# VectorE's second zero point of context rows ahead of the split of the maxima (iterations 9 to 15)

## What is computed

```python
x = x + attn(layernorm(x), Wq, Wk, Wv, Wo)       # 32 query heads, 8 key heads of 32, causal, softmax
x = x + fake_quant(layernorm(x)) @ fake_quant(ctx)  # ctx: 2 x 1024 x 1024
x = x + q8_8_linear(layernorm(x), weight, bias)

def fake_quant(x, scale, zp):
    q = clip(round(x / scale + zp), 0, 255)
    return (q - zp) * scale
```

## Time and profile before

| | us |
|---|---|
| median of 3 runs (480.33 to 484.75) | 481.57 |
| the profiled execution, its time | 483.82 |
| its span, first to last instruction | 481.9 |
| TensorE busy | 438.9 |
| VectorE busy | 379.4 |
| ScalarE busy | 299.4 |
| GpSimd busy | 288.4 |

### The profile page before, as it was taken

One profiled execution on the slowest core, in us unless ns is written; L12 is line 12 of the kernel. 1 busy time (PEld: TensorE's weight loads), 2 busy tenths in 40 slices (PEclk: granted clock), 3 DMA queues, 4 the chain that ended last, 5 costly groups with the idle time before them and its releaser, 6 DMA issues.

```text
span 481.9 us, 9721 instructions
## 1 busy us (share of the span) xinstructions
PE 438.9 (91%) x3730; PEld 241.3 (50%) x3730; DVE 379.4 (79%) x961; ACT 299.4 (62%) x302; POOL 288.4 (60%) x157
## 2 busy tenths in 40 slices
PE   0799997998899999999999999998998999899886
PEld 0676453545455555555554555445543444446442
DVE  5899862978888989888978888888287468799775
ACT  3775262223778777778777797779744312797632
POOL 5002662144899999999987877879730980707000
PEclk9999998999999999999999999999999999999999
DMA  8663486412231111110153213332177010000044
GB/s 332 215 220 110 147 277 199 174 45 79 78 123 32 47 47 55 57 50 31 47 176 111 81 37 107 111 110 94 40 275 264 30 38 29 1 1 2 2 177 177
DMA packets 21042, 50.93 MB, mean 106 GB/s; under 512 B 4736, under 2 KB 10112, under 8 KB 19712
## 3 DMA queue, kind: packets, MB, share of 16 engines
q1 hardware_dynamic: 19696, 41.79, 25.4%
q10 hardware_dynamic: 1296, 8.45, 5.0%
HBM read 40.67 MB, written 9.44 MB: 104 GB/s over the span
## 4 chain that ended last, share of the span: by engine, by line
PE 50%; DVE 21%; POOL 12%; ACT 7%; issue 5%; DMA 5%; SPq 0%; ACTq 0%; DVEq 0%; POOLq 0%
PE ps L1466 11%; PE ps L1372 8%; PE ps L1289 8%; PE ps L1617 5%; PE ps L1353 5%; PE ps L1334 4%; POOL more L1206 4%; DVE stat L769 3%; ACT s1reg L566 3%; POOL s1reg L1206 3%; POOL wkv L1206 2%; PE ps L1572 2%; PE ps L1355 2%; DVE qstack L957 2%; DVE ps L829 2%
## 5 line engine op out<-in xcount | busy, mean ns | idle before, releaser
L829 DVE CUSTOM_DVE_ANT_0 ps<-ps,causal 128x512 f32<-128x512 f32 (+3 forms) x256 | 120.4, 511 | 19.3 <-PE ps L1334 17.3
L566 ACT ACTIVATE s1reg<-ps 128x1280 f32<-128x1280 f32 x64 | 78.8, 1231 | 48.5 <-PE ps L1355 48.5
L1289 PE MATMUL ps<-xT,wqx 128*128 128x512 f16 x384 | 96.5, 384 | 0.0
L1466 PE MATMUL ps<-wo_reg,xT 128*128 128x512 f16 x384 | 93.0, 379 | 0.0
L1334 PE MATMUL ps<-kreg,qstack 96*128 96x512 f16 (+3 forms) x256 | 60.5, 301 | 10.0 <-DVE mt L829 6.7
L1353 PE MATMUL ps<-qstack,kreg 98*128 98x512 f16 (+3 forms) x256 | 57.2, 301 | 0.5 <-ACT s1reg L566 0.5
L1289 PEld LDWEIGHTS ps<-xT,wqx 128*128 128x128 f16 x384 | 37.2, 99 | 37.3 <-issue 2.2
L1466 PEld LDWEIGHTS ps<-wo_reg,xT 128*128 128x128 f16 x384 | 36.5, 97 | 36.6 <-issue 0.2
L1187 POOL TENSOR_TENSOR s1reg<-s1reg 128x512 f32<-128x512 f32 x11 | 16.0, 1451 | 63.0 <-DVE s1reg L818 62.9
L1206 POOL TENSOR_TENSOR s1reg<-s1reg 128x1280 f16<-128x1280 f32 x19 | 49.8, 2622 | 6.2 <-ACT s1reg L572 6.0
L1206 POOL TENSOR_TENSOR wkv<-s1reg,wkv 128x1280 f16<-128x1280 f32 x18 | 47.2, 2628 | 7.5 <-ACT wkv L572 7.5
(11 more groups left out here) (134 smaller groups left out, 929.1 us busy)
## 6 DMA issues: line engine op xcount, KB each, us to landing
s1reg<-in_weights ACTq DMA_DIRECT2D x8, 1024.0 KB, 5.1
s1reg<-in_ctx SPq DMA_DIRECT2D x16, 512.0 KB, 4.2
qstack<-rope_scratch SPq DMA_DIRECT2D x48, 128.0 KB, 2.6
rope_scratch<-s1reg SPq DMA_DIRECT2D x40, 128.0 KB, 2.2
qstack<-in_x SPq DMA_DIRECT2D x8, 512.0 KB, 5.4
s1reg<-in_x SPq DMA_DIRECT2D x16, 256.0 KB, 3.1
out<-s1reg SPq DMA_DIRECT2D x7, 512.0 KB, 2.7
s1reg<-in_L_ffn_weight SPq DMA_DIRECT2D x5, 512.0 KB, 6.0
```

The source lines that it names most:

```text
L566: nc.scalar.activation(ebuf[:, j % 2, :], st_ps[:, 0:SCORES], ACT.Exp, scale=EXP_SCALE, bias=P_LOG_SCALE).then_inc(e_done, 1)
L829: last = nc.vector.tensor_tensor_reduce(part, part, causal[:, T - w:T], 1.0, LOWEST, ALU.add, ALU.max, mt[:, G % 2, h, qt:qt + 1])
L1289: last = mm(out_ap, w(ws, k), xT[:, xs, KT * b + k, :], start=(k == 0 and n == 0), stop=(k == KT - 1 and n == 2))
L1466: last = mm(ps[:, bank, :], xT[:, os, KT * b + k, t], wo_sb[:, ws, 4 * h:4 * h + 4, k, :], start=(k == 0 and n == 0), stop=(k == KT - 1 an ...
```

## The change

In the loop of VectorE the zero point of the even tile, with its two waits, goes from behind maximum 6 to ahead of the split. No instruction is added or removed, and the other engines' instructions and waits are the same.

```diff
                 maxes(G, 3, 6)
-                if G < NG - 1:
-                    split_max(G + 1)
-                maxes(G, 6, 7)
                 if g >= 1:
                     dve.wait_ge(st_done, G * 4)
                     ctx(g * 2 - 2, 0)
-                maxes(G, 7, 11)
+                if G < NG - 1:
+                    split_max(G + 1)
+                maxes(G, 6, 11)
```

## The result

The changed kernel takes 480.41 us (median of 21 runs, 477.39 to 483.22), the kernel before 483.16 us (21 runs, 479.95 to 485.86). The ratio, which is worked out from the single runs and is not the quotient of the two medians, is 0.9948, with a 95% interval of 0.9926 to 0.9970: 2.5 us faster, between 1.4 and 3.6; the medians differ by 2.75. One run of the third, 521.49 us at a granted clock of 0.85 where all others had 0.99 to 1.00, is left out of its median and ratio.

The account below looks back on a forecast made before the run. VectorE's even zero point, waiting for GpSimd, was taken to hold up TensorE. 0.73 + 4 x 0.65 to 0.72 + 0 to 0.1 gave 3.3 to 3.7, taken as 3.4 us: 478.2 from 481.57; 8 in 10: 475.9 to 480.6.

Parts of the forecast that it names:

- What bounds the kernel: VectorE's even zero point waits for GpSimd's low half and holds the maxima TensorE needs; 15.04 us an iteration.
- V: Landmark of each iteration: the start of the denominators on TensorE; V to V was 15.04 us.
- The zero point takes 0.74 in its new place, the split costs nothing: VectorE, iterations 9 to 13: zero point starts before GpSimd, 0.74 us instead of 1.55; split 0.16 late, cost nothing.
- The slower rival: Zero point comes after GpSimd has started its low half; unit 10 1.38 us later, 6.9 us in all, 488.5; chance 0.04.
- The ring of 14.32 or 14.39 us: V, exponential 2, ScalarE's run, GpSimd's last low half, V again: limits each iteration's gain to 0.65 to 0.72 us.
- The full gain: Rival: V does not hang on the low halves, so TensorE's 5.0 us all arrive, 476.6 us; chance 0.14.
- The 0.07: Extra time of TensorE's denominators after a wait, 1.27 against 1.20 us, added to 14.32 to give 14.39.
- The odd zero point: VectorE's unmoved zero point: takes about 1.4 us instead of 0.74, priced at 0 to 0.1 us an iteration.
- the chain over L566, L572 and L1205: Sign in the profile after: the chain in 260 to 330 us runs over these lines in place of L957.
- V(9) to V(10), 0.73: First step: V(10) can't be before 261.57 because of GpSimd's last low half, so it gains 0.73 us, not 1.20.
- TensorE alone needs 14.09: TensorE's iteration without waiting for GpSimd: 15.04 less 0.95 us gained at unit 10.
- From the stage to the predicted time: Whole kernel: 3.4 us gained between V(9) and V(15), taken from the median of 481.57, gives 478.2 us.

Follow-up runs that it names:

- the third: The changed kernel measured a third time, with no further edit, beside the kernel before: 479.61 against 482.88 us, ratio 0.9922.
- the second profile of before: The kernel before measured against itself, nothing changed: 483.40 against 482.88 us, ratio 1.0016.
- the heads alone: Kernel before with ScalarE's high half of the head outputs moved behind exponential 3's high half from iteration 9 on: 483.66 against 481.97 us, ratio 1.0039.
- the two repeats: The changed kernel measured again twice, no further edit, against the kernel before: ratios 0.9963 and 0.9922.

## Where the prediction was right, and where it was not

*What bounds the kernel:* right. The zero point at its old place waited for the low half; shown by moving it behind the split (15.69 us from V to V), and by shortening the low half in place (14.40).

*The zero point takes 0.74 in its new place, the split costs nothing:* right, 0.75, and maximum 6 still waits 0.30 for TensorE. The slower rival's mechanism is real (2.62 us, 15.69), but its condition was not met: the zero point comes 0.56 us ahead of the low half (284.49 and 285.05).

*The ring of 14.32 or 14.39 us:* right, 14.40 measured in each of the iterations. The full gain did not come because of this ring: 0.38 us of TensorE's gain became a wait for GpSimd. The 0.07 between the two sums is no cost of a wait, though. It is the difference of the two landmarks named above:

```profile
277.27 0.39 PE L1372 MATMUL ps<-more,ones_h 128*32 128x512 f16 x1
```

Counted from this first matmul, exponential 2 (283.13) came 5.86 us after V(11) before the change too, and the 32 matmuls take 1.27 us with and without a wait ahead of them. So the ring is 5.86 + 5.56 + 2.62 + 0.35 = 14.39. The odd zero point's 1.48 (1.4 expected) and the chain over L566, L572 and L1205 are as written.

*V(9) to V(10), 0.73:* mis-sized, by what was taken as the step before. It was 15.46 in the profile of before, in which ScalarE's bytes waited for their transfer; the prediction kept the last low half where that wait had put it. The row of ScalarE's timeline of before, after which exponential 2 came 6.30 us after V(9) and not 5.86:

```profile
251.92 1.24 ACT L585 ACTIVATE wkv<-s1reg,qs 128x1024 uint8<-128x1024 f32 x1 [0.41 <-DMA s1reg<-in_ctx]
```

In the second profile of before there was no such wait, and the step took 15.04; with the heads alone the wait was 0.25 and the step 15.30. After the change it took 14.40, and 14.51 in its third run. The term is worth 0.5 to 1.1 us, depending on the execution, and the sum of the stage 3.2 to 3.7 us: 3.3 to 3.7 had been forecast.

*TensorE alone needs 14.09:* wrong by 0.14 (13.95). Up to unit 8 (10.69 us after V(11)) TensorE's iteration is the same before and after, so nothing came from exponential 0; all of it came at units 9 and 10. Maximum 8 started 0.42 us behind unit 8 (287.68 and 287.26) and not 0.53, and unit 10 followed unit 9 directly, 1.09 us earlier after V than before where 0.95 was worked out. This would have made the full gain larger; it didn't touch the forecast.

*From the stage to the predicted time:* this is the step that failed, in two terms. The first is the size: 3.4 us off a base of 481.57 gave 478.2, and 480.41 was measured, 2.2 more and within the range only by 0.2. 1.6 of the 2.2 is the base: 481.57 was the median of three runs, and 21 runs of the same kernel have 483.16. The other 0.6 is the gain, 2.75 between the medians where 3.4 was taken, though the stage itself gave its 3.2 to 3.7: the sum took for granted that the stage's gain reaches the median whole, and had no term for the first 130 us, in which V(1) scatters by 5 us. How much of the 0.6 these took is known only as far as the clocks above tell. The second is what a measurement can tell: the prediction called one per cent, 4.8 us, about the least that can be told from no change, and so named "within 1%" as likeliest, while its own sum of 3.4 us implied a gain clear of zero. The measurement told a gain of 2.5 us with an interval of 1.1 us to either side, and the two repeats, with wider intervals (1.6 and 1.5 us), were clear of zero as well. That the time came inside the range is owed to its width, and not to this step.

## What to carry to other kernels

When one instruction has two or three lengths in a trace, look for what runs on the other engine at its start: its place should be chosen by who is first at the shared resource, and a place at which it starts 1.1 us later can cost more than the old one did. Before counting what a removed wait gives back, walk the next ring (here V, exponential 2, ScalarE, the last low half, V) and take the smaller gain. If the same loop runs elsewhere in the trace without the cost that is to go, its period there is the forecast: here 14.40 us stood in seven of the first eight steps. Then look in that ring for the next edit, which was worth nothing on its own and 1.4 to 1.9 us in this stage behind the first. Compare stages by landmarks in the traces when the part before them scatters by more than the change is worth, and whole times between runs of the same granted clock. Take the base of a forecast from more than three runs, and what a measurement can tell from the interval of one with as many runs.

## What the runs showed of the hardware

VectorE's subtraction of 128 x 1024 bytes to float16 takes 0.74 to 0.75 us when nothing holds it, and if GpSimd's instruction has started first it ends 0.54 to 0.56 us after that one (1.38 to 2.62 us long in the cases shown here). The exception is a start in the last 0.13 us of GpSimd's instruction, as at 291.25 before the change: it takes its plain 0.74, so it is held until a little before the recorded end and no longer. The other way round GpSimd's instruction, started while VectorE's ran, was 0.05 us longer for an overlap of 0.19 us by the records, 0.44 longer for 0.59 (the heads alone, low half 3 of iteration 14) and 0.45 longer for 0.59 (the low half of the head outputs, 1.61 after the change, 1.16 where it was first). This is what the Trainium skill (SBUF — State Buffer, "Who interferes with whom") says of the shared port pair: issue order decides who blocks. The trace agrees, in both orders.

I had not expected that the first 130 us of the same work would scatter by 5 us (V(1) from 128.78 to 133.99) while each stage of the following 350 us repeats within 0.5 us from execution to execution, nor that stretches of some 3 us at half the clock would stand ahead of V(1) in eight of eleven profiles, once or twice, and in the other three not at all.
